# A two-layer attention and experts kernel: a new order of its steps, maxima by half units, loads by thirds, padded operands

## What is computed

```python
x = x + xattn(layernorm(x), ctx_768, ...)      # softmax(q k^T / sqrt(8)) v, then a projection
x = x + ffn(layernorm(x), ...)

# ffn:
h = rmsnorm(x, ln1_w)
q, k, v = h @ Wq + bq, h @ Wk + bk, h @ Wv + bv
q, k = rmsnorm(rope(q), qn_w), rmsnorm(rope(k), kn_w)
out = causal_attention(q, k, v)
x = x + (out * sigmoid(out @ Wg + bg)) @ Wo + bo
h2 = rmsnorm(x, ln2_w)
top1 = argmax(h2 @ Wr + br)
u = h2 @ W1[top1] + b1[top1]
y = (u[:256] * sigmoid(u[256:])) @ W2[top1] + b2[top1]
return x + y
```

## Time and profile before

| | us |
|---|---|
| median of 3 runs | 284.21 |
| runs | 284.21, 284.7, 280.51 |
| span of the profiled execution | 280.0 |
| busy: PE, DVE, ACT, POOL | 191.0, 156.2, 113.4, 109.8 |
| moved by DMA | 25.65 MB in 25294 packets |
| mean granted clock of PE | 0.840 |

### The profile page before, as it was taken

One profiled execution on the slowest core, in us unless ns is written; L12 is line 12 of the kernel. 1 busy time (PEld: TensorE's weight loads), 2 busy tenths in 40 slices (PEclk: granted clock), 3 DMA queues, 4 the chain that ended last, 5 costly groups with the idle time before them and its releaser, 6 DMA issues.

```text
span 280.0 us, 4383 instructions
## 1 busy us (share of the span) xinstructions
PE 191.0 (68%) x1426; PEld 114.3 (41%) x1426; DVE 156.2 (56%) x429; ACT 113.4 (41%) x200; POOL 109.8 (39%) x177
## 2 busy tenths in 40 slices
PE   0350575999987974996677697998965227339991
PEld 0220322655643532552343244543332217339881
DVE  1313489589899656478578666774241732024551
ACT  2221020466653662562353274657543113035650
POOL 1401047270082162173168063536241057723454
PEclk9999985599997797799689689999795557757996
DMA  7986886633420135034252233202110113430100
GB/s 181 191 206 183 226 247 189 159 118 120 111 62 0 35 88 151 0 108 105 59 163 50 60 105 108 62 0 96 40 37 0 39 51 107 93 43 15 33 25 0
DMA packets 25294, 25.65 MB, mean 92 GB/s; under 512 B 3600, under 2 KB 21980, under 8 KB 24264
## 3 DMA queue, kind: packets, MB, share of 16 engines
q1 hardware_dynamic: 23544, 22.44, 29.2%
q0 software_dynamic: 1296, 2.50, 3.9%
q10 hardware_dynamic: 432, 0.43, 0.7%
HBM read 15.98 MB, written 9.70 MB: 92 GB/s over the span
## 4 chain that ended last, share of the span: by engine, by line
PE 37%; DVE 19%; DMA 15%; issue 8%; POOL 6%; ACT 6%; another core or an unknown queue 4%; SPq 2%; POOLq 0%; ACTq 0%; DVEq 0%
PE S L1139 9%; PE O L1139 9%; PE MXX L1139 9%; DMA KA<-k_rows 7%; DVE NEGM L848 6%; PE MS L1139 5%; DMA X<-in_x 3%; DMA QA<-MTS 2%; PE MS L1370 2%; DMA k_rows<-PT 1%; ACT SJ L713 1%; POOL R L496 1%; POOL PT L501 1%; DMA GR<-h_rows,IDX 1%
## 5 line engine op out<-in xcount | busy, mean ns | idle before, releaser
L848 DVE TENSOR_REDUCE NEGM<-MXX 128x2 f32<-128x512 f32 (+1 forms) x112 | 74.2, 686 | 29.9 <-PE MXX L1139 28.7
L734 ACT ACTIVATE EX<-S 128x1024 f32<-128x1024 f32 x64 | 58.4, 915 | 37.8 <-PE S L1139 37.3
L1139 PE MATMUL MXX<-KA,QA 96*128 96x256 bf16 (+1 forms) x256 | 49.9, 300 | 26.1 <-DMA KA<-k_rows 17.2
L1139 PEld LDWEIGHTS MXX<-KA,QA 96*128 96x128 bf16 x256 | 21.8, 109 | 50.6 <-DVE NEGM L848 22.7
L1139 PE MATMUL S<-QA,KA 96*128 96x256 bf16 (+1 forms) x176 | 38.6, 327 | 0.9 <-DMA QA<-MTS 0.9
L603 POOL TENSOR_SCALAR_AFFINE_SELECT EX<-EX 128x512 f32<-128x512 f32 x32 | 20.2, 636 | 27.2 <-ACT EX L734 27.2
L496 POOL TENSOR_TENSOR R<-QKF,PT 128x512 f32<-128x512 f32 x6 | 6.9, 1157 | 51.0 <-ACT PT L685 51.0
L1139 PEld LDWEIGHTS S<-QA,KA 96*128 96x128 bf16 x176 | 17.6, 106 | 12.1 <-issue 4.1
L1139 PE MATMUL O<-EX,VA 128*32 128x256 f32 x256 | 21.8, 414 | 0.0
L956 DVE SCALAR_TENSOR_TENSOR AJ<-S,WJ,SJ 128x128 f32<-128x128 f32 x30 | 9.1, 345 | 21.6 <-ACT SJ L713 18.6
L713 ACT ACTIVATE SJ<-S,WJ 128x128 f32<-128x128 f32 x30 | 9.4, 364 | 26.7 <-PE S L1139 10.9
(11 more groups left out here) (161 smaller groups left out, 303.3 us busy)
## 6 DMA issues: line engine op xcount, KB each, us to landing
q_rows<-PT SPq DMA_DIRECT2D x24, 192.0 KB, 2.4
QA<-q_rows SPq DMA_DIRECT2D x8, 576.0 KB
k_rows<-PT SPq DMA_DIRECT2D x12, 192.0 KB, 3.9
KA<-k_rows SPq DMA_DIRECT2D x4, 576.0 KB
W<-in_w SPq DMA_DIRECT2D x8, 258.0 KB, 3.1
W<-in_w SPq DMA_DIRECT2D x8, 128.0 KB, 2.8
h_rows<-HR SPq DMA_DIRECT2D x4, 256.0 KB, 2.1
KA<-in_ones_row SPq DMA_DIRECT2D x3, 192.0 KB
```

The costliest lines, as they stand in the source:

```text
L734: act.activation(EX[g % PRING][:, 0:w], S[g % 2][:, 0:w], ACT.Exp).then_inc(probs, 1)
L848: dve.tensor_reduce(out=NEGM[:, q, heads[0]:heads[-1] + 1], in_=MX[g % 2][:, 0:len(heads) * w].rearrange("p (h t) -> p h t", t=w), axis=AX ...
L1139: return nc.tensor.matmul(out_, lhsT, rhs, start=start, stop=stop, **kw)
```

## The change

Each step now has a place of its own for each engine on a grid of quarter beats. The projections of layer 1 come ahead of the grid, for all four batches, k of batch 0 first. The maxima of a unit go back in two halves, and scores start 7 beats after the first bank. SP loads QA and KA in three parts each, each behind its own store; parts of q are stored once and read three times over. QA and KA have 128 rows: DVE clears rows 64 to 127, the ones lie in rows 96 and 97, the maxima too, and the scores contract all 128 rows while the maxima contract 96. Newton's steps move to POOL, the copies into VA to ACT (the bias of the values goes through the projection into PBV), Z and ZB to beat 35. The layernorm in front of qkv subtracts the mean before and scales after the matmul. PT, QKF, R1 and XNT have two buffers; GR and WJ lie in KA's buffers. Routing and experts are unchanged.

```diff
+MROWS = KROWS + 2
+HALF = H // 2
...
-        PAUSE = 4
-        AT1 = {"pj": 7, "hz": 8, "hz_t": 9, "qkv": 10, "squares": 11, "newton1": 11,
-               "newton2": 11.5, "newton3": 12, "qn_t": 13.5, "split2": 14.5}
-        AT2 = {"gate": 7.5, "wo": 9, "xp_t": 10, "h2": 11, "router": 11.5}
-        BOTH = {"o_sb": 4.5, "o_t": 5, "on_t": 6}
+        PAUSE = 2
+        LAG = 7
+        STEP = 4
+        AT1 = {"pj": 19.5, "x1": 19.75, "rstd2": 20.75, "hz_t": 21.25, "ht": 21.5, "qkv": 22.25, "qkvs": 22.5,
+               "squares": 22.75, "ssq": 24, "newton": 24.25, "qn": 26.25, "qn_t": 26.75, "qkf": 27, "rest1": 27.75,
+               "part2": 28.5, "part3": 29, "z": 35}
+        AT2 = {"gate": 19.5, "tanh": 19.75, "gt": 20.25, "wo": 20.75, "xp": 21, "ss3": 21.5, "rms3": 21.75,
+               "xp_t": 22, "xpt": 22.25, "h2": 23.25, "router": 23.25, "lg": 23.75}
+        BOTH = {"o_sb": 17, "o_t": 17.5, "on": 17.75, "on_t": 18.5, "ont": 18.75}
...
+        def attention_at(now, behind=0.0):
             for e in range(NE):
-                beat = BEATS * k + i - behind - start(e) - 2 * BEATS - LAG
+                beat = now - behind - start(e) - LAG
...
+            def q_store(e, c):
+                sp.dma_start(q_rows[e, c], PT[e % 2][:, c, 0, :]).then_inc(q_out[c], 16)
+            def k_load(e, c):
+                nk, k_e = heads_of_k(e), k_rows[e] if e < B else k2_rows[e - B]
+                sp.wait_ge(k_out[c], 16 * (e + 1))
+                sp.dma_start(KA[e % RING][c:ROWS:NPART, 0:nk, :].rearrange("p h t -> p (h t)"),
+                             k_e[c].rearrange("i (d h) t -> (i d) (h t)", h=nk)).then_inc(k_stacked[e % RING], 16)
+            def q_load(e, c):
+                n = NPART * HD
+                sp.wait_ge(q_out[c], 16 * (e + 1))
+                sp.dma_start(QA[e % RING][n * c:n * c + n, :, :].rearrange("p h t -> p (h t)"),
+                             q_rows[e, c].rearrange("(d h) t -> d (h t)", h=H)[:, None, :]
+                             .broadcast_to([HD, NPART, H * T])).then_inc(q_stacked[e % RING], 16)
+            def stack(e):
+                if e >= RING:
+                    sp.wait_ge(scores, BEATS * (e - RING + 1))
+                for c, ready in enumerate((part1, part2, part3)):
+                    sp.wait_ge(ready, 2 * e + 2)
+                    q_store(e, c)
+                    k_store(e, c)
+                    if c:
+                        q_load(e, c - 1)
+                        k_load(e, c - 1)
+                q_load(e, NPART - 1)
+                k_load(e, NPART - 1)
+            def maxima_in(e, half):
+                sp.wait_ge(mts, 2 * e + half + 1)
+                sp.dma_start(QA[e % RING][KROWS:MROWS, HALF * half:HALF * half + HALF, :]
+                             .rearrange("p h (q t) -> p (h q) t", q=TT), MTS[:, half, :]).then_inc(m_rows[e % RING][half], 16)
...
+            for e in range(4, NE):
+                if e + 1 < NE:
+                    stack(e + 1)
+                maxima_in(e, 0)
+                maxima_in(e, 1)
+                if e + 1 < NE:
+                    expert_weights(e + 1)
...
+            def newton(b):
+                pool.wait_ge(guess, b + 1)
+                for step in range(NEWTON):
+                    link(pool.tensor_tensor(RT[:, :], RQ[:, :], RQ[:, :], ALU.mult))
+                    link(pool.tensor_tensor(RT[:, :], RT[:, :], SSQ[:, :], ALU.mult))
+                    link(pool.tensor_scalar(RT[:, :], RT[:, :], -0.5, 1.5, ALU.mult, ALU.add))
+                    last = pool.tensor_tensor(RQ[:, :], RQ[:, :], RT[:, :], ALU.mult)
...
+            def clear_padding(i):
+                for A in (QA[i], KA[i]):
+                    last = dve.memset(A[P // 2:P, :, :].rearrange("p h t -> p (h t)").bitcast(fp32), 0.0)
+                last.then_inc(padded, 1)
+
+            clear_padding(0)
+            dve.wait_ge(ld["x0"], 16)
+            ln1_stats(0)
+            ln1(0)
+            dve.wait_ge(ld["x1"], 16)
+            for b in range(1, B):
+                ln1_stats(b)
+            rest_part(1, 1)
+            ln1(1)
+            last_part(1, 1)
+            ln1(2)
+            rest_part(0, 2)
+            last_part(0, 2)
+            ln1(3)
+            clear_padding(1)
+            clear_padding(2)
...
-                        last = mm(S[g % 2][:, T * j:T * j + T], ka[:, 4 * u + j, P * kt:P * kt + P], qa[:, 4 * u + j, :])
+                        last = mm(S[g % 2][:, T * j:T * j + T], ka[0:P, 4 * u + j, P * kt:P * kt + P],
+                                  qa[0:P, 4 * u + j, :])
```

1308 lines of the change are left out of this document (668 added, 640 removed).

## The result

Measured side by side, four runs each:

| | before | after |
|---|---|---|
| median, us | 283.57 (280.51 to 284.7) | 270.52 (267.01 to 271.32) |
| ratio | | 0.954, 95% interval 0.944 to 0.964 |
| profiled execution: time, span | 284.2, 280.0 | 270.42, 268.7 |

The account below looks back on a forecast made before the run. The prediction held the loop bound by in-order waits as much as by work. 280.0 less 7.1 (start) and 32.4 (loop and attention) gave a span of 240.5; 4.2 on top gave 245 us, range 227 to 269 for 8 in 10.

Parts of the forecast that it names:

- The start: Before the loop: less traffic and loads in thirds bring the first bank at 22.5 us for 29.6, bounds 18 and 27.
- Beats 0 to 8: Loop's beginning, banks alone: 16 maxima in 10.3 us plus 0.9 for two halves, 11.2 us for 15.5.
- Beats 8 to 16: Attention starts with PE's clock probably at 1.2 GHz: three beats at 2.8, five at 1.6, 16.4 us for 17.6.
- the largest term and only a floor is in the rows: In the loop, separate places on the quarter-beat grid remove in-order waits; only the busiest engine's work was known as a floor.
- SP's queue: Each unit issues 14 DMAs for 10, 1.6 us more per 8 beats; slack some 2 beats, thinner on first units.
- Newton on POOL: 12 small operations per batch take 3.7 us, meeting causal selects only for batch 3, about 1.5 us once.
- The wait for unit 4's stack: Before layer 2: the 5.80 us wait for loading KA is gone; beats 24 to 34 take 22.0 us.
- Padded operands at nothing: Scores contracting 128 rows for 96 cost nothing; if time went by rows, 0.2 us a beat, 13 us in all.
- Rival 1: In the loop, waits come back elsewhere and beats keep their mean of 2.34 us: 267 us; chance 0.22.
- Rival 2: Loop closer to the floor, beats at 1.9 us, and half the unknown 10.60 us gone: 233 us; chance 0.18.
- rival 4: SP's added issues and POOL's Newton eat the gain, every loop beat 2.6 us: 285 us; chance 0.06.
- Rival 3: Gaps keep PE's clock at 1.2 GHz, beats of 3.1 us: 318 us if all 66 ran so; chance 0.06.

Follow-up runs that it names:

- d1: Changed kernel with the stack loads of units 3 to 7 cut to one row each and Newton's operations left out: 241.5 us, 0.909 of the kernel before.
- set 5: Fifth set of follow-up kernels, run on one chip beside the kernel before, which took a median of 268.9 us there.
- a5: Changed kernel with attention and all steps behind it one beat later (8 beats behind the maxima for 7): 269.9 us, 1.008 of the kernel before.
- The two controls: The changed kernel itself, measured again in the third and fourth sets: 272.4 and 272.1 us, 0.977 and 0.972 of the kernel before.
- b2: Changed kernel with the loads of the stacks of units 3 to 7 cut to one row each: 264.2 us, 0.946 of the kernel before.
- c2: Changed kernel with Newton's 12 operations on POOL replaced by a single one whose result nobody reads: 266.7 us, 0.952 of the kernel before.
- a1: Changed kernel with the transfers of the maxima's rows issued by ACT instead of SP: 269.7 us, 0.959 of the kernel before.
- a3: Changed kernel with two rows of maxima issued by SP ahead of a stack's loads instead of behind them: 269.1 us, 0.961 of the kernel before.
- a2: Changed kernel with Newton's 12 operations per batch back on DVE in one piece: 283.6 us, 1.012 of the kernel before.
- a8: Changed kernel with Newton on DVE, four operations at each of three places half a beat apart: 265.3 us, 0.986 of the kernel before.
- b4: Kernel before the change with only Newton's steps moved from DVE to POOL: 285.5 us, 1.019 of the kernel before.
- a6: Changed kernel with a pause of 4 beats between the layers instead of 2: 262.7 us, 0.979 of the kernel before.
- a7: Changed kernel with scores contracting the 98 rows that carry data instead of all 128: 258.7 us, 0.959 of the kernel before.
- sets 2 and 3: Second and third sets of follow-up kernels, each run beside the kernel before, which took a median of 268.8 us in the second.

## Why the prediction was wrong, step by step

The loop was the term that failed; the others hold to a few microseconds, one of them by luck.

| step of the sum | forecast | changed kernel | with both causes out (d1) |
|---|---|---|---|
| first bank | 22.5 | 25.2 | 26.8 |
| beats 0 to 8 | 11.2 | 15.5 | 15.6 |
| 8 to 16 | 16.4 | 15.8 | 15.4 |
| 16 to 24 | 16.0 | 21.5 | 17.2 |
| 24 to first bank of unit 4 | 22.0 | 25.2 | 22.2 |
| 34 to 50 | 34.4 | 39.4 | 35.4 |
| 50 to 66 | 32.0 | 39.0 | 33.5 |
| last bank to one-hot | 25.5 | 25.8 | 25.1 |
| routing and experts | 60.5 | 61.3 | 47.6 (set 5) |

The changed kernel's loop is 156.3 us for 132.0 forecast, 24.3 us more. The start adds 2.7, tail and experts 1.1, so that the span is 28.2 us longer than the 240.5 of the sum. The time around the span was 1.7 us for the 4.2 taken; this error the other way leaves 25.7 (270.4 for 244.7), by luck. Each unit's last maxima bound the rows of the table, but for the first bank of unit 4; the first row is the first maximum. With both causes out, 16.9 of the 24.3 us are gone; of the 7.4 that stay, 4.4 are in beats 0 to 8.

*The start.* The maxima came at 25.2, inside the bounds 18 to 27, the first bank at 24.6. The order held, with stores of 2.59 us (k) and 3.46 (q) where 2.4 was taken, and 4.0 us from the issue of the last load, at 20.6, to the bank, where 2.9 was taken. SP's issues were mis-sized: loads of a third took it 0.65 to 0.77 us each, not 0.4. The memsets were six at 1.765 us, near the 1.9 taken:

```profile
L1049 DVE MEMSET QA<- 64x2048 f32 x3 | 5.3, 1765 | 2.1 <-PEq L1593 1.3 <-issue 0.9
```

The rule of the Trainium skill, "VectorE: DVE Perf Modes", section "Zero memsets can be issued as uint32 (trn2)", gave an estimate of 2.1; here the measurement decides, 1.765. As to the number of engines that a load uses, the rule of the Trainium skill, "DMA: Bandwidth & Descriptors", section "Why a DMA increments its semaphore by 16 and not by 1", says that the semaphore gets one update for each engine used, behind one at once for all the rest. The traces agree with the prediction's reading: one and 8 updates for each load of q, one and 12 for each of the old loads. What the smaller number costs no run isolates.

*Beats 0 to 8.* Mis-sized by 4.3 us, d1's too, and by 1.1 to 4.5 in all profiles. DVE's maxima did come back to back, as the forecast has them, up to the fifteenth, which ends at 36.2. Then the first scores, which lag 7 puts ahead of the last banks, wait on PE for their row (issued at 33.4, 3.56 us), and DVE waits behind PE:

```profile
37.04 1.03 PE L1213 MATMUL S<-QA,KA 128*128 128x256 bf16 x4 [1.61 <-DMA QA<-MTS]
38.54 0.69 DVE L935 TENSOR_REDUCE NEGM<-MXX 128x2 f32<-128x512 f32 x1 [2.38 <-PE MXX L1213]
```

With the scores a beat later (a5) all maxima of unit 0 come back to back, and it takes 12.3 us.

*Beats 8 to 16.* 15.8 for 16.4 is luck. The forecast explained its number by a clock at the lower level; the clock was 1.00, and a row's 5.04 us stood there instead. The two controls took 17.1 and 18.1 us.

*The beats from 16 on.* The step that failed is "the largest term and only a floor is in the rows": that places of their own bring a beat from 2.34 near to 2.0. It took 2.36. The lengths as such can be had: without the loads and without Newton's chain the 42 beats from 24 on take 91.1 us for the 88.4 forecast, where the changed kernel takes 103.6. What was wrong is to think that places of their own were enough to come near them. The sum put the stalls of the old windows down to steps that stand in one place; the runs show 8 us of the changed kernel's to be the loads of the stacks (b2), 5 the chain through POOL (c2), 12 to 18 both together (d1).

*SP's queue.* The forecast saw `maxima_in` behind the stack's loads and allowed for it in three beats of 2.8 us. On the later units it counted issues and slack in SP's queue: four more issues of 0.4 us, 1.6 us a unit. In fact six loads of 0.71 us stand for two of 0.33, which makes 3.6 us more a unit, and SP's issuing became part of the chain (14.8 us in the loop, 13.9 and 21.4 in the controls). The rows were late by what the DMA engines had to do beside them: a queue of their own did not help (a1), a place ahead of the loads did for the row (a3), smaller loads did for the time (b2).

*Newton on POOL.* 4.1 us where 3.7 was taken, but called hidden save for the causal selects of one batch. It lies on the path, for a third of its length. That leaving DVE pays was right (a2 and a8), though not in the old grid (b4).

*The wait for unit 4's stack.* "The 5.80 us wait is gone" was wrong: a load of 3.91 and two stores of 3.12 and 2.86 us stand there, and the stage took 3.2 us more than forecast; with small loads and no Newton (d1) it took the 22.2 us of the forecast. *The pause* counts, as supposed (a6). *Padded operands at nothing*: right (a7). *Tail and experts*: 25.8 for 25.5 and 61.3 for 60.5, with the unknown wait kept, as it was right to do for this set.

*Rivals.* Rival 1, the waits come back elsewhere, gave 267 us with beats of 2.34. The measured 270.5 with beats of 2.36 is this rival, but for the later first bank. Its chance of 0.22 was too low: nothing in the rows showed that a wait taken from its place is gone for good. Two of the prediction's own signs of being wrong came: 2.45 us a beat from 34 to 66, and scores that wait for their rows. Rival 2 would have needed shorter beats, and rival 4 beats of 2.6. Rival 3, the clock, is refuted as a large cause: 0.93 in the loop after for 0.86 before, and loops of about the same length.

## What to carry to other kernels

Before giving a grid's places credit for idle time, name for each stall the resource that ends it and what that resource does next; if it is shared bandwidth or one engine's chain, moving the waiter only moves the wait. A tiny transfer that the next beat needs is late when a burst is under way beside it, so issue it ahead of the burst (2.0 us for 6.0 in a3), and do not expect another queue to help; then see what meets the burst in its place. When a large transfer is cut into several, price the issues too. Measure two suspected causes out together as well as apart: here the loop fell by more than the two single effects.

## What was not expected of the hardware

- 8 KB of rows took 1.9 to 2.1 us to land in quiet beats (nine of sixteen in the changed kernel), and 5.0 to 7.6 us beside stack loads and weights, from SP's queue or ACT's.
- Issuing a load of a third cost SP 0.71 us on average, a load of a single row some 0.25.
- The granted clock hardly matters to d1_loads_and_newton: with mean clocks of 0.932 and 0.868 it had spans of 238.9 and 239.2 us.
- The unknown wait of 10 to 12 us in the expert stage is there for every kernel of some sets and for none of others (60.3 to 61.6 us against 47.6 and 47.7). What it is stays open; sets 2 and 3, one without it and one with it, ran on the same chip.
